# Moving second-stage transposes one piece ahead in an embedding-interaction kernel, with warm-up matmuls and a reordered one-hot

## The chip, the cores and the metric

One core of one Trainium2 chip runs the kernel. The metric is device time in microseconds of one execution; lower is better. Inputs lie in HBM before the clock starts, and the output (512 numbers) is written back to HBM.

## The reference

A batch of 512 samples has 128 dense features and 26 table indices each. Every index picks a row of 128 numbers out of its table, so a sample has 26 embedding vectors and, with the dense features, 27 vectors. All their pairwise dot products feed a small tower of three layers:

```python
e = stack([tbl_f[ids[:, f]] for f in range(26)], axis=1)      # 512 x 26 x 128
sd = einsum('bfd,bd->bf', e, dense)                            # 26 per sample
ss = einsum('bfd,bgd->bfg', e, e); pairs = ss[:, iu, ju]       # 325 per sample
h = concat([dense, sd, pairs, dense], axis=1)                  # 512 x 607
h = maximum(h @ W_top1 + b_top1, 0)                            # 607 -> 512
h = maximum(h @ W_top2 + b_top2, 0)                            # 512 -> 256
y = h @ W_top3                                                 # 256 -> 1
```

## The kernel before

The kernel writes each engine's instruction stream by hand and ties them with semaphores. It has two stages.

**Gathers.** Sixteen of the tables (MAIN) are read row by row with indirect DMAs issued by GpSimd (POOL), line 294. There are 64 of them, four for each of 16 blocks of 32 samples, called b0 to b15. They land in the ring `rows`, which holds three blocks; the gathers of block n+3 wait until the transposes of block n are done (`filled`, line 293). TensorE (PE) then transposes the four 128x128 pieces of a block against the identity `ident` into a PSUM bank `stage` (function `transposes`, line 325), and ScalarE (ACT) copies them into the big table of vectors `ET` (`empty_stage`, line 470). The two stage banks are used in turn.

**Look-ups, first stage.** The other ten tables (ONE, about 1000 rows each) are loaded whole by SyncE's queue (SP). ACT casts each table to an upper part (`upper_part`, lines 457 and 459), VectorE (DVE) makes the rest, the lower part (`lower_part`, "split", line 558), and one-hot matrices of the indices (`make_onehot`, line 552). PE multiplies them (`look_up`, line 342). The tables come in six groups, SIDE = [[0],[1,2],[3,4],[5,6],[7,8],[9]], and each group takes eight chunks k = 0..7; a chunk is two matmuls of 512 columns for each table of the group. The results go by turns to the banks `gram` and `hidden`, and ACT takes them out (`take_look_up`, lines 480, 482). The dictionary AMID (line 200) says after which chunk (group, k) PE places the transposes of the dense features and of b0 to b7. ACT's stream follows the same dictionary.

**Second stage.** The samples are cut into nine pieces p: seven of 64 samples, two of 32. `gram_piece` (line 371) multiplies each sample's 27 vectors by themselves, 32x27 results a sample; the trace shows two matmul records for each, so 128 a piece of 64. DVE and ACT move the result from PSUM to `Z` (lines 568 and 492), DVE folds it with a mask (579, 586), and `layers(p)` runs the part of layers 1 and 2 (lines 387, 398, 413, 415) whose inputs are ready: nothing for p = 0 and 1, two columns of layer 1 from p = 2 on, layer 2 one piece later. Layer 3 is line 599 on DVE. The order on PE in piece p is: gram_piece(p), the transposes in SOON[p], layers(p), the transposes in LATER[p] (lines 429 to 435). A gram piece waits until ACT has emptied the stage bank of its last block (line 353); its first one waits for the last look-up (line 355).

The two dictionaries of the second stage are:

```python
SOON = {1: ["b8"], 2: ["b9"], 3: ["b10"], 4: ["b11"], 5: ["b12"]}
LATER = {5: ["b13"], 6: ["b14"], 7: ["b15"]}
```

At the start ACT's queue issues three small DMAs, the last of them (line 505) the bias of layer 1, transposed on the way in elements of four bytes. DVE's order in a group g of two tables is: both splits, then the eight one-hots (lines 615 to 619).

Of the kernel before, what the change touches and what calls it, by code (L numbers as in the profile page):

```python
# [11 lines left out]
P = 128  # L12
# [7 lines left out]
HC = H1 // P  # L20
# [14 lines left out]
KR = 8  # L35
RAW = 3

SIDE = [[0], [1, 2], [3, 4], [5, 6], [7, 8], [9]]
RING = 8


BS = 32
# [32 lines left out]
def group_of(i):  # L75

    return next(g for g, side in enumerate(SIDE) if i in side)
# [29 lines left out]
def dlrm_tower(nc, x, out):  # L107
    ctx = ExitStack()
    with ctx:
        def sb(name, shape, dt=F32):  # L110
            return ctx.enter_context(nc.sbuf_tensor(name, shape, dt))

        def pb(name, shape):
            return ctx.enter_context(nc.psum_tensor(name, shape, F32))

        def sem(name):
            return ctx.enter_context(nc.semaphore(name))
# [10 lines left out]
        part = sb("part", [P, 4, 2, KR * D], FP32R)  # L128
        onehot = sb("onehot", [P, RING, 2 * B], FP32R)
        ident = sb("ident", [P, P])  # L130
# [5 lines left out]
        b1c = sb("b1c", [P, HC])  # L136
# [12 lines left out]
        second = [pb(f"second{i}", [P, 512]) for i in range(2)]  # L149
# [11 lines left out]
        w1d_in = sem("w1d_in")  # L161
# [7 lines left out]
        ident_ready = sem("ident_ready")  # L169
# [28 lines left out]


        AMID = {(0, 7): ["dense"], (1, 3): ["b0"], (2, 1): ["b1"], (2, 5): ["b2"], (3, 1): ["b3"],  # L200
                (3, 6): ["b4"], (4, 3): ["b5"], (4, 7): ["b6"], (5, 7): ["b7"]}

        SOON = {1: ["b8"], 2: ["b9"], 3: ["b10"], 4: ["b11"], 5: ["b12"]}
        LATER = {5: ["b13"], 6: ["b14"], 7: ["b15"]}
        STAGED = [s for g, k in sorted(AMID) for s in AMID[g, k]] + [s for n in range(NP) for s in SOON.get(n, []) + LATER.get(n, [])]

        def bank_of(name):

            return stage[STAGED.index(name) % 2]

        def filled(name):

            return staged, STAGED.index(name) + 1
# [5 lines left out]
        def look_banks(g):  # L219

            return [b[:, :] for b in (gram if g % 2 == 0 else hidden)]
# [87 lines left out]
        def _(pe):  # L309
# [18 lines left out]
            def look_up(g):  # L328
# [4 lines left out]
                for k in range(KR):  # L333
                    pe.wait_ge(onehot_ready, KR * g + k + 1)
                    for j, i in enumerate(SIDE[g]):
# [5 lines left out]
                        for n in range(2):  # L341
                            last = pe.matmul(look_banks(g)[j], part[:, i % 4, n, D * k:D * (k + 1)],  # L342
                                             onehot[:, (KR * g + k) % RING, B * j:B * (j + 1)],
                                             start=(k == 0 and n == 0), stop=(k == KR - 1 and n == 1))
# [74 lines left out]
            def layers(p):  # L419

                for t, c in layer2_of(p):
                    layer2(t, c)
                for t, c in layer1_of(p):
                    layer1_dense(t, c)
                    layer1(t, c)

            for g in range(len(SIDE)):
                look_up(g)
            for p in range(NP):
                gram_piece(p)  # L430
                for name in SOON.get(p, ()):
                    transposes(name)
                layers(p)
                for name in LATER.get(p, ()):
                    transposes(name)
# [12 lines left out]
        @block.scalar  # L448
        def _(act):
            def upper_part(i):  # L450

                act.wait_ge(table_in[i], 16)
                if i >= 4:

                    act.wait_ge(chunk_done, KR * (group_of(i - 4) + 1))
                if i == 0:
                    act.copy(part[:, 0, 0, 2 * D:], raw[:, 0, 2 * D:]).then_inc(hi_ready, 1)
                else:
                    act.copy(part[:, i % 4, 0, :], raw[:, i % RAW, :]).then_inc(hi_ready, 1)  # L459

            def empty_stage(name):

                act.wait_ge(*filled(name))
                bank = bank_of(name)
                if name == "dense":
                    act.copy(denseT[:, :], bank[:, :])
                    act.copy(ETv[:, :, DENSE], bank[:, :]).then_inc(stage_taken, 1)
                else:
                    n = int(name[1:])
                    act.copy(ETv[:, BS * n:BS * (n + 1), 0:NM],  # L470
                             bank[:, :].rearrange("d (b v) -> d b v", v=NM)).then_inc(stage_taken, 1)

            def take_look_up(g):

                act.wait_ge(chunk_done, KR * (g + 1))
                for j, i in enumerate(SIDE[g]):
                    if i == NO - 1:

                        for at in (slice(0, P), slice(P, B)):
                            act.copy(ETv[:, at, V_ONE[i]], look_banks(g)[j][:, at]).then_inc(look_taken, 1)  # L480
                    else:
                        act.copy(ETv[:, :, V_ONE[i]], look_banks(g)[j]).then_inc(look_taken, 1)  # L482

            def move_gram(p):
                act.wait_ge(gram_done, p + 1)
                t = PIECES[p][0] // P
                if t >= ZT:

                    act.wait_ge(h1_done, HC * (t - ZT + 1))
                for i in (2, 3):  # L490
                    for dst, src in z_moves(p, (i,)):
                        last = act.copy(dst, src)  # L492
                    if i == 2:
                        for name in SOON.get(p, ()):
                            empty_stage(name)
                last.then_inc(gram_act, 1)

            def take_odd(t, c):

                act.wait_ge(h1_done, HC * t + c + 1)  # L500
                act.activation(h1T[:, t % 2, c, :], layer1_bank(t, c), ACT.Relu, bias=b1c[:, c:c + 1]).then_inc(h1_odd, 1)  # L501

            act.dma_start(rowid[:, :], x["rowid"]).then_inc(rowid_in, 16)
            act.dma_start(b2s[:, :], x["b_top2"].rearrange("(o n) -> o n", o=1)).then_inc(b2_in, 16)
            act.dma_start(b1c[:, :], x["b_top1"].rearrange("(c p) -> p c", p=P), allow_slow_non_contiguous=True).then_inc(w1d_in, 16)
            act.wait_ge(dve_consts, 1)
            act.activation(warm[:, :], zero[:, :], ACT.Identity, bias=zero[:, :])
            act.wait_ge(b2_in, 16)
            act.copy(b2h[:, 0, :], b2s[:, :]).then_inc(b2_high, 1)
            act.wait_ge(head_in, 16)  # L510
            act.copy(part[:, 0, 0, 0:2 * D], raw[:, 0, 0:2 * D]).then_inc(hi_ready, 1)
            for i in range(4):
                upper_part(i)
            for g in range(len(SIDE)):
                for k in range(KR):
                    if k == KR - 1:
                        take_look_up(g)
                    for name in AMID.get((g, k), ()):
                        empty_stage(name)
                for i in range(4, NO):  # L520
                    if group_of(i - 4) == g:
                        upper_part(i)
                if 1 <= g <= T:

                    t = g - 1
                    if t == 0:
                        act.wait_ge(look_taken, 3)
                        act.wait_ge(*emptied("dense"))
                    of = ETv[:, P * t:P * (t + 1), :]
                    act.copy(of[:, :, NV:NV + 3], of[:, :, LATE:NV])  # L530
                    act.copy(of[:, :, NV + 3:VP], of[:, :, LATE:LATE + VP - NV - 3]).then_inc(et_again, 1)
            act.wait_ge(w1d_in, 32)
            for p in range(NP):
                move_gram(p)
                if layer1_of(p):
                    take_odd(*layer1_of(p)[1])
                for name in LATER.get(p, ()):
                    empty_stage(name)
            for c in (1, 3):
                take_odd(T - 1, c)  # L540

        @block.vector
        def _(dve):
            def make_onehot(g, k):
                m = KR * g + k
                if k == 0:
                    dve.wait_ge(ids_in[g], 16)
                if m >= RING:

                    dve.wait_ge(chunk_done, m - RING + 1)  # L550
                w = B * len(SIDE[g])
                dve.tensor_scalar(onehot[:, m % RING, 0:w], ids16[:, B * SIDE[g][0]:B * SIDE[g][0] + w],  # L552
                                  rowid[:, k:k + 1], None, ALU.is_equal).then_inc(onehot_ready, 1)
# [59 lines left out]
                make_onehot(0, k)  # L613

            for g in range(1, len(SIDE)):
                for i in SIDE[g]:
                    lower_part(i, slice(0, KR * D)).then_inc(lo_ready, 1)
                for k in range(KR):
                    make_onehot(g, k)
            dve.wait_ge(b2_high, 1)  # L620
            dve.tensor_tensor(b2h[:, 1, :], b2s[:, :], b2h[:, 0, :].bitcast(F32), ALU.subtract).then_inc(b2_low, 1)
# [69 lines left out]
```

## Time and profile before

| what | value |
| --- | --- |
| median of three runs | 132.18 us (131.85 to 134.35) |
| the profiled execution's own time | 132.72 us |
| its span, first to last instruction | 130.9 us |
| PE busy / DVE / ACT / POOL | 94.0 / 73.7 / 61.8 / 67.5 us |
| mean granted TensorE clock | 0.896 of full |

The span is what the trace shows; 1.8 us of the execution's own time lie around it. PE's busy time includes matmuls that overlap, so it isn't PE at its peak. "Issue" is time in which an engine waited for nothing that the profile shows.

### The profile page before, as it was taken

How to read it: one execution, taken by the hardware profiler on the slowest of the kernel's cores; microseconds unless marked ns; L12 is line 12 of the kernel's file. 1: busy time of each engine (PE TensorE's matmuls, PEld its weight loads, DVE VectorE, ACT ScalarE, POOL GpSimd, SP SyncE). 2: the span in 40 equal slices, each digit the busy share in tenths (PEclk: the TensorE clock that was granted, in tenths of full speed). 3: DMA queues.
4: the chain of work that ended last, by engine and by line, in shares of the span. 5: the costliest groups of instructions: out<-in, count | busy, mean ns of one | idle time of the engine just before them, and what ended most of it. 6: DMA issues, size and time to landing. Idle time of an engine off the chain costs nothing.

```text
span 130.9 us, 3331 instructions
## 1 busy us (share of the span) xinstructions
PE 94.0 (72%) x1420; PEld 78.2 (60%) x1420; DVE 73.7 (56%) x170; ACT 61.8 (47%) x131; POOL 67.5 (52%) x70
## 2 busy tenths in 40 slices
PE   0089899999969999000547459397784997897892
PEld 0157688888858887000436349286674796786780
DVE  1387999999997835000008927264370731974621
ACT  3435591966908506300308909164370904964410
POOL 2878888787888787770831725538172560000000
PEclk9999999999999999965557756999999559999999
DMA  2999965947996121220110110102011110000000
GB/s 53 242 379 367 272 242 185 267 115 179 381 372 207 44 60 40 63 59 21 44 41 8 45 40 25 49 16 60 25 38 43 25 40 25 0 5 0 8 0 1
DMA packets 6849, 13.37 MB, mean 102 GB/s; under 512 B 2353, under 2 KB 3506, under 8 KB 6834
## 3 DMA queue, kind: packets, MB, share of 16 engines
q1 hardware_dynamic: 4112, 8.95, 21.4%
q0 software_dynamic: 2048, 4.20, 11.2%
q8 instruction: 11, 0.18, 0.6%
q10 hardware_dynamic: 674, 0.01, 0.3%
q14 instruction: 4, 0.03, 0.1%
HBM read 13.15 MB, written 0.00 MB: 100 GB/s over the span
## 4 chain that ended last, share of the span: by engine, by line
PE 44%; POOL 17%; issue 15%; DMA 7%; another core or an unknown queue 6%; ACT 6%; DVE 2%; DVEq 0%; ACTq 0%
POOL rows L294 17%; PE gram L371 12%; PE hidden L398 8%; PE second L415 6%; PE gram L342 6%; DMA rows<-in_tables_gather,idx 5%; PE stage L325 5%; PE hidden L387 3%; PE hidden L342 2%; ACT Z L492 2%; ACT ET L470 2%; ACT ET L482 2%; PE second L413 2%; DVE Z L568 2%
## 5 line engine op out<-in xcount | busy, mean ns | idle before, releaser
L294 POOL DMA_INDIRECT rows<-in_tables_gather,idx x64 | 66.8, 1044 | 39.0 <-issue 17.4
L568 DVE COPY Z<-gram 32x112 f32<-32x112 f32 (+3 forms) x72 | 23.0, 320 | 35.5 <-PE gram L371 34.6
L371 PE MATMUL gram<-ET 128*32 128x27 f32 x1024 | 17.0, 207 | 25.8 <-issue 12.8
L492 ACT COPY Z<-gram 32x112 f32<-32x112 f32 (+1 forms) x72 | 23.2, 322 | 23.7 <-PE gram L371 22.9
L371 PEld LDWEIGHTS gram<-ET 128*32 128x32 f32 x1024 | 14.1, 123 | 29.4 <-issue 26.0
L552 DVE TENSOR_SCALAR onehot<-ids,rowid 128x1024 fp32r<-128x1024 int16 (+1 forms) x48 | 28.7, 659 | 5.1 <-DMA ids<-in_ids_one 2.1
L342 PE MATMUL gram<-onehot,part 128*128 128x512 f32 x80 | 22.5, 434 | 6.6 <-DVE part L558 6.2
L342 PEld LDWEIGHTS gram<-onehot,part 128*128 128x128 f32 x80 | 16.4, 211 | 10.7 <-DVE onehot L552 6.2
L342 PE MATMUL hidden<-onehot,part 128*128 128x512 f32 x80 | 19.7, 397 | 0.6 <-issue 0.6
L342 PEld LDWEIGHTS hidden<-onehot,part 128*128 128x128 f32 x80 | 14.6, 188 | 3.7 <-issue 0.8
L558 DVE TENSOR_TENSOR part<-raw,part 128x1024 fp32r<-128x1024 f32 (+2 forms) x11 | 12.1, 1123 | 3.1 <-issue 2.4
L398 PE MATMUL hidden<-Z,W1s 128*128 128x128 f32 x84 | 13.2, 301 | 0.6 <-DVE Z L579 0.6
L398 PEld LDWEIGHTS hidden<-Z,W1s 128*128 128x128 f32 x84 | 12.2, 219 | 0.8 <-DVE Z L579 0.8
L459 ACT CAST part<-raw 128x1024 fp32r<-128x1024 f32 x9 | 9.4, 1070 | 5.2 <-DMA raw<-in_tables_one 4.3
L470 ACT COPY ET<-stage 128x512 f32<-128x512 f32 x16 | 9.5, 592 | 4.8 <-issue 4.6
L325 PE MATMUL stage<-ident,rows 128*128 128x128 f32 x64 | 10.8, 295 | 1.0 <-DMA rows<-in_tables_gather,idx 1.0
L415 PE MATMUL second<-W2s,h1T 128*128 128x256 f32 x32 | 10.2, 436 | 0.0
L325 PEld LDWEIGHTS stage<-ident,rows 128*128 128x128 f32 x64 | 8.0, 150 | 2.5 <-issue 1.4
L482 ACT COPY ET<-gram 128x512 f32<-128x512 f32 x5 | 5.3, 1145 | 6.9 <-PE hidden L342 5.6
L415 PEld LDWEIGHTS second<-W2s,h1T 128*128 128x128 f32 x32 | 5.8, 206 | 1.6 <-ACT h1T L501 0.4
L501 ACT ACTIVATE h1T<-hidden,b1c 128x128 f32<-128x128 f32 x7 | 2.6, 367 | 7.3 <-PE hidden L398 7.2
L387 PE MATMUL hidden<-denseT,W1e 128*128 128x128 f32 x28 | 6.0, 306 | 0.0
(38 smaller groups left out, 42.2 us busy)
## 6 DMA issues: line engine op xcount, KB each, us to landing
raw<-in_tables_one SPq DMA_DIRECT2D x9, 512.0 KB
ids<-in_ids_one SPq DMA_DIRECT2D x4, 256.0 KB, 5.5
rows<-in_tables_gather,idx POOLq DMA_INDIRECT x64
W1s<-in_W_pairs SPq DMA_DIRECT2D x1, 768.0 KB
W1d<-in_W_dense SPq DMA_DIRECT2D x1, 512.0 KB
W2s<-in_W_top SPq DMA_DIRECT2D x1, 512.0 KB
raw<-in_tables_one SPq DMA_DIRECT2D x1, 384.0 KB
ids<-in_ids_one SPq DMA_DIRECT2D x2, 128.0 KB, 3.6
```

The source lines that it names most:

```text
L294: pool.indirect_dma_start(out=rows[:, m % ROWS_RING, :], out_offset=None, in_=x["tables_gather"], in_offset=bass.IndirectOffsetOnAxis(ap=i ...
L325: last = pe.transpose(bank[:, P * k:P * (k + 1)], rows[:, (GB * n + k) % ROWS_RING, :], ident[:, :])
L342: last = pe.matmul(look_banks(g)[j], part[:, i % 4, n, D * k:D * (k + 1)], onehot[:, (KR * g + k) % RING, B * j:B * (j + 1)], start=(k == ...
L371: last = pe.matmul(gram[p % 2][32 * i:32 * i + 32, NV * j:NV * (j + 1)], ET[:, VP * b:VP * (b + 1)], ETv[:, b, 0:NV], start=True, stop=True)
L387: pe.matmul(layer1_bank(t, c), W1e[:, P * c:P * (c + 1)], denseT[:, P * t:P * (t + 1)], start=True, stop=False)
L398: last = pe.matmul(layer1_bank(t, c), W1s[:, s, P * c:P * (c + 1)], Z[:, t % ZT, s, :], start=False, stop=(s == 0))
L415: last = pe.matmul(at, h1T[:, t % 2, c, :], W2s[:, c, :], start=False, stop=(c == HC - 1))
L470: act.copy(ETv[:, BS * n:BS * (n + 1), 0:NM], bank[:, :].rearrange("d (b v) -> d b v", v=NM)).then_inc(stage_taken, 1)
L492: last = act.copy(dst, src)
L552: dve.tensor_scalar(onehot[:, m % RING, 0:w], ids16[:, B * SIDE[g][0]:B * SIDE[g][0] + w], rowid[:, k:k + 1], None, ALU.is_equal).then_inc ...
L558: return dve.tensor_tensor(part[:, i % 4, 1, cols], raw[:, i % RAW, cols], part[:, i % 4, 0, cols].bitcast(F32), ALU.subtract)
L568: last = dve.tensor_copy(dst, src)
```

## The change

Five edits. (1) PE runs ten 128x128 matmuls of the identity with itself before the first look-up. (2) The bias of layer 1 is laid out by the host as it stands in SBUF, so its DMA is a plain one. (3) In a group of two tables DVE makes the one-hot of chunk 0 between the two splits. (4) The transposes of b4, b5 and b6 move to later chunks of the look-ups. (5) In the second stage the transposes of b8 to b13 stand behind the gram pieces 0 to 5, one piece earlier each; b13, which stood behind layers(5), now stands ahead of them. b14 and b15 stay.

```diff
+WARM = 10
         AMID = {(0, 7): ["dense"], (1, 3): ["b0"], (2, 1): ["b1"], (2, 5): ["b2"], (3, 1): ["b3"],
-                (3, 6): ["b4"], (4, 3): ["b5"], (4, 7): ["b6"], (5, 7): ["b7"]}
-
-        SOON = {1: ["b8"], 2: ["b9"], 3: ["b10"], 4: ["b11"], 5: ["b12"]}
-        LATER = {5: ["b13"], 6: ["b14"], 7: ["b15"]}
+                (4, 1): ["b4"], (4, 4): ["b5"], (5, 1): ["b6"], (5, 7): ["b7"]}
+
+        SOON = {p: [f"b{p + 8}"] for p in range(6)}
+        LATER = {6: ["b14"], 7: ["b15"]}
...
+            pe.wait_ge(ident_ready, 1)
+            for n in range(WARM):
+
+                pe.matmul(second[0][:, 0:P], ident[:, :], ident[:, :], start=True, stop=True)
             for g in range(len(SIDE)):
                 look_up(g)
...
-            act.dma_start(b1c[:, :], x["b_top1"].rearrange("(c p) -> p c", p=P), allow_slow_non_contiguous=True).then_inc(w1d_in, 16)
+            act.dma_start(b1c[:, :], x["b_top1"]).then_inc(w1d_in, 16)
...
             for g in range(1, len(SIDE)):
-                for i in SIDE[g]:
+                for n, i in enumerate(SIDE[g]):
                     lower_part(i, slice(0, KR * D)).then_inc(lo_ready, 1)
-                for k in range(KR):
+                    if n == 0:
+
+                        make_onehot(g, 0)
+                for k in range(1, KR):
                     make_onehot(g, k)
...
-        "b_top1": np.ascontiguousarray(inputs["b_top1"]), "W_top2": np.ascontiguousarray(inputs["W_top2"]),
+        "b_top1": np.ascontiguousarray(np.asarray(inputs["b_top1"]).reshape(HC, P).T), "W_top2": np.ascontiguousarray(inputs["W_top2"]),
```

## Rows read from the trace of the kernel before

**Rows 1.** The page, busy tenths in 40 slices of 3.27 us, and TensorE's granted clock.
```profile
PE   0089899999969999000547459397784997897892
POOL 2878888787888787770831725538172560000000
PEclk9999999999999999965557756999999559999999
```

**Rows 2.** The waits: engine, line, waited for; us in total, times, longest.
```profile
PE gram L371 <- issue: 12.8, 20, 1.2
...
POOL rows L294 <- PE stage L325: 17.0, 5, 4.6
...
POOL rows L294 <- remote: 3.0, 1, 3.0
```

**Rows 3.** POOL's timeline, first gather of a block: start, us, what, idle before.
```profile
71.41 0.94 POOL L294 DMA_INDIRECT rows<-in_tables_gather,idx  x1 [4.56 <-PE stage L325]
...
79.62 0.94 POOL L294 DMA_INDIRECT rows<-in_tables_gather,idx  x1 [3.52 <-PE stage L325]
...
87.06 0.94 POOL L294 DMA_INDIRECT rows<-in_tables_gather,idx  x1 [2.75 <-PE stage L325]
...
102.62 0.94 POOL L294 DMA_INDIRECT rows<-in_tables_gather,idx  x1 [3.36 <-PE stage L325]
```

**Rows 4.** Windows, line 371 alone: span, PE and PEld busy (records), clock, DMA, GB/s.
```profile
62.17:66.85 4.68, 2.36 (x67) 1.61 (x67) 0.50 0.18 46
66.85:71.41 4.56, 2.72 (x189) 2.73 (x189) 0.62 0.07 20
...
79.62:84.31 4.69, 1.23 (x46) 0.76 (x46) 0.90 0.17 45
...
99.25:102.62 3.37, 1.01 (x87) 0.98 (x87) 0.77 0.10 24
102.62:107.31 4.69, 0.00 (x0) 0.00 (x0) 0.50 0.17 42
```

**Rows 5.** PE's timeline in the second stage.
```profile
62.35 0.85 PE L371 MATMUL gram<-ET 128*32 128x27 f32 x46 [10.01 <-ACT ET L480]
...
67.84 2.72 PE L371 MATMUL gram<-ET 128*32 128x27 f32 x189 [1.12 <-issue]
...
86.72 0.50 PE L413 MATMUL second<-b2h,ones 1*128 1x256 f32 x2
...
89.99 0.50 PE L371 MATMUL gram<-ET 128*32 128x27 f32 x34
...
100.29 1.01 PE L371 MATMUL gram<-ET 128*32 128x27 f32 x87 [1.20 <-issue]
...
102.28 0.79 PE L413 MATMUL second<-b2h,ones 1*128 1x256 f32 x2
...
108.09 0.60 PE L325 MATMUL stage<-ident,rows 128*128 128x128 f32 x4
109.36 1.29 PE L371 MATMUL gram<-ET 128*32 128x27 f32 x128 [0.68 <-ACT ET L470]
```

**Rows 6.** PE's timeline in the look-ups.
```profile
6.23 2.05 PE L342 MATMUL gram<-onehot,part 128*128 128x512 f32 x4 [6.23 <-DVE part L558]
...
38.49 0.63 PE L325 MATMUL stage<-ident,rows 128*128 128x128 f32 x4 [1.03 <-DMA rows<-in_tables_gather,idx]
...
51.74 0.60 PE L325 MATMUL stage<-ident,rows 128*128 128x128 f32 x4
```

**Rows 7.** ACT's timeline at the end of the look-ups.
```profile
50.38 2.05 ACT L482 COPY ET<-gram 128x512 f32<-128x512 f32 x2 [5.63 <-PE hidden L342]
...
61.87 1.08 ACT L480 COPY ET<-hidden 128x128 f32<-128x128 f32 x2 [8.22 <-remote]
```

**Rows 8.** DVE's timeline, second split of group 1.
```profile
12.44 1.22 DVE L558 TENSOR_TENSOR part<-raw,part 128x1024 fp32r<-128x1024 f32 x1 [0.73 <-issue]
```

**Rows 9.** The chain in order of time: start, us, what.
```profile
105.08 0.43 PE hidden L387 x2
```

## The prediction

> **What bounds the kernel now.** I read the busy tenths first, then the waits, then PE's and POOL's timelines side by side. The tenths [rows 1] show three parts: look-ups with a dense PE to about 52 us, an empty PE for three slices, and a second stage from 62 us in which PE is half busy and POOL works in bursts. The granted clock falls to half twice, around 57 to 80 us and at 101 to 108 us, each time after PE had been thin or idle.
>
> In the second stage two waits are large and belong together [rows 2]. POOL waits 17.0 us in all, five times, for PE's transposes: a block of gathers may start only when the block three before it is transposed. And PE's gram matmuls have 12.8 us of idle "issue", in 20 gaps, for which no semaphore is to blame. Laid on top of each other, the timelines say what the gaps are. The windows in [rows 4] have POOL's bursts as their boundaries. A burst is four gathers and takes 4.68 us. While one runs, a gram piece gets through its first 34 to 47 records at a free pace and then nearly stops (46 in all in 79.62:84.31, 67 in the first burst); with POOL idle 189 pass in 2.72 us. Behind the first burst, which ends at 66.85, the gram runs free again at 67.84; behind the fifth, which ends at 99.25, at 100.29 [rows 4, 5]. The three between are the same: 0.97 to 1.04 us behind the burst's end, five times out of five. The wide matmuls of the layers don't stop so: in 102.62:107.31 POOL gathers, PE has no gram, and the layers run through.
>
> So the second stage is one loop over two engines. Transposes of a block release a burst (4.68), the gram piece that falls beside it is held to burst end + 1.0, its rest takes about 1, its transposes and the wake-up of POOL 0.85 (full clock) or 1.32 (half). The loop's period is what [rows 3] show: 8.21, 7.44, then 7.51, then 8.05 us (102.62 - 87.06 = 15.56 for the last two). Two things escape the loop now. Piece 1 follows piece 0 in the same free run of 189 records, beside no burst. And the last burst (b15's gathers, from 102.62) lies beside layers(5).
>
> In front of it, PE's last look-up record and b7's transposes end at 52.34 [rows 6], but ACT takes the last table only at 61.87 [rows 7], and POOL, which needs b7's transposes, is held 3.0 us until 62.17 [rows 2]. Group 4's result too is taken late, at 50.38 after 5.63 us of waiting [rows 7], though the records have group 5's matmuls running from 48 us on. PE's completions reach the others late here, and they all come through once POOL has gone quiet at 62.17 - 3.0 = 59.17. The records don't say why. I take it for the same coupling of PE to the gathers as in the gram.
>
> **The change part by part.** The sum is made against the span of the profiled execution, 130.9 us, whose own time is 132.72; that is 0.54 above the median of 132.18, so a difference is added to the median.
>
> *Second-stage transposes one piece ahead.* Call X the start of the first burst of this stage (now 62.17). Piece 0 is unchanged: it ends at X + 6.77 (68.94 now: 4.68 + 0.99 + 61 records in 1.10). Today piece 1 follows at once. After the change b8's transposes do, and POOL's next burst starts at X + 6.77 + 1.32 = X + 8.09, instead of X + 9.24. That is 1.15 us earlier, and it is the gain. The price is that piece 1 now runs beside this burst. It has at most 0.3 us before POOL wakes, some 20 records, and then the usual 46; it needs 128, so it is held. Then each piece has a burst:
> - to b8's burst: 8.09
> - piece 1, no layers beside it, as piece 2 today: 8.21
> - piece 2, no layers between it and its burst, the same: 8.21
> - piece 3: 7.44; piece 4: 7.51
> - piece 5 to its end: 8.05 - 1.32 = 6.73
> Together X + 46.2 for the end of piece 5, which today is at 101.30 = X + 39.1. From there to piece 6, today takes 8.06 (101.30 to 109.36): b12's transposes, layers(5) 102.28 to 108.09, b13's transposes and 0.68 of waiting for ACT to copy them [rows 5]. Afterwards b13's are the only ones and ACT's copy lies beside layers(5): transposes 0.6 (full) to 1.05 (half) and layers 3.3 (as 86.72 to 89.99, full clock) to 5.8 (half, as now). I take the middle, 5.4, because today's half clock there comes after a thin piece 5 and the new piece 5 is as thin, but starts from another moment. So piece 6 starts at X + 51.6, against X + 47.2 now: +4.4, with ends +2.9 and +5.9. A few tenths come back because piece 1 starts with some records done: -0.2. From piece 6 on nothing is changed; b14 and b15 stay where they were.
>
> *Look-ups.* b4's transposes wait 1.03 us for their gathers [rows 6]; three chunks later they don't: -1.03 on PE, or nothing if the engine behind it is late. The one-hot between the splits fills DVE's idle 0.73 before the second split [rows 8], one one-hot being 0.66: PE can begin group 1 with the first table, and DVE, which is busy without a gap from there to 42 us, is 0.66 earlier throughout. The ten identity matmuls: the nearest row has two records (one such matmul) in 0.43 us at half clock [rows 9], so 4.3 us from about 1.5, done at 5.8, and PE has nothing to do until 6.23 anyway [rows 6]. Ends: +0.5 if they run over, and at best they let group 0 run at full clock (its first four took 2.05 us, half a microsecond each, where a pair of records is half as long at full clock); but group 1 can't be complete before its second split, 12.44 + 1.22 = 13.66 [rows 8], so that up to 2 us gained in group 0 become 0.7 at most behind it. The bias DMA falls from elements of 4 bytes; bounds 0 to -0.3 on the first table's arrival. Together PE's look-ups end 1.3 to 3 us earlier.
>
> What of it arrives? X doesn't hang on PE's records but on when the completions come through, and they do when POOL goes quiet. POOL is busy without a gap from 3 to 59 us at its own pace and isn't sped up by any edit. Two ways: completions come through as now, a little sooner because fewer are left: X -0.3 to -1. Or b6, now two chunks later, is still outstanding when POOL wants it, one burst and a start ahead of 59.17, at 54.48. Then POOL goes quiet there for 1 to 2 us, everything comes through, and b7 never holds it: its two bursts follow each other and X falls at 60.5 to 61.5. No lateness at all would give 59.47, the lowest X can be: -2.7. I take -1.2; the range is 0 to -2.7.
>
> Sum: +4.4 - 0.2 - 1.2 = +3.0 us. Span 133.9, own time 135.7, against the median 135.2. A measurement of this kernel can tell about 2%, 2.6 us, from no change.
>
> The Trainium skill (SBUF — State Buffer, section "SBUF: two separate sides") says that DMA ports and engine ports are disjoint, that a DMA can't be slowed by a compute operation nor the other way round, and that PE never waits on anyone. By that rule the gaps of rows 4 would have another cause and piece 1 would stay as cheap as it is. The trace speaks against it with five coincidences of 1.0 us, so the sum doesn't use it; it is the second rival's ground.
>
> **The rivals.**
> *A. Piece 1 slips through.* If the hold needs more of POOL's burst than I think (in piece 0 the free pace ends at 63.20, 1.03 us behind the burst's start) and piece 1's 128 records, 1.84 us at the free pace, are nearly out by then, b9's transposes follow at once and two bursts run back to back beside piece 2. Piece 2 then ends at X + 8.09 + 9.7 + 2.0 = X + 19.8 instead of X + 23.2. That is -3.4, so -0.4 in all: 131.8. For it: piece 1 starts ahead of the burst. Against: pieces 0 and 2 to 5 stop after 34 to 47 records wherever they start in the burst, so it is a count and not a time.
> *B. The gaps aren't tied to the gathers (the faster side).* Then the transposes ahead cost nothing, POOL's 17.0 us of waiting shrink, b13's 0.68 us of waiting for ACT goes, and the look-ups' 1.3 to 3 us reach X. Gain 2.9 to 4.6: about 128.5. If the late completions vanish too, up to 8 us more. It decides if the windows with gathers show piece 1 complete. Against it stand rows 4.
> *C. Nothing arrives from the look-ups and layers(5) run at half clock:* +5.9 - 0.2 = +5.7, 137.9; the forecast's upper end.
>
> **How the numbers follow.** Forecast with its clock variants 0.55 (its own range 133.5 to 137.9), A and mixtures near no change 0.25, B 0.2. Slower by over 2% is over 134.8: 0.43, from most of the forecast. Faster by over 2%: 0.19, B. Within: 0.38. The range goes from 129.5, which leaves out the better half of B, to 138.0.
>
> **What would show it.** Right: piece 1 stops after 46 to 80 records and runs free 1.0 us behind the end of b11's gathers; six bursts of which five gate a gram piece behind piece 0; POOL's last burst starts near 100, and PE's piece 6 behind 111; POOL's waiting for transposes falls while gram's "issue" grows by about 4 us. The first burst of the stage starts near 61. PE's first table starts at 6.2 still, group 1 before 14.38, no wait of b4's transposes. Wrong: piece 1's records within 2.5 us of each other beside gathers, or X below 59.4, or completions of the look-ups that come in time.

## The result, and the profile after

The changed kernel has a median of 137.55 us (135.84 to 139.52, four runs) beside 132.3 us for the kernel before. The ratio is 1.033, with a 95% interval of 1.020 to 1.045: slower, by over 2%. Two of the four runs, the profiled one among them (138.0 us), lie over 1.5% above the fastest and aren't in the ratio; the granted clock of all four is the same to 0.003. The forecast was 135.2 us and slower. By the ratio the forecast's own baseline of 132.18 becomes 136.5, which is 1.3 us above the forecast; the median is 2.35 above it. Both are inside the range.

The page: busy tenths of PE and POOL in 40 slices (now 3.41 us each) and the granted clock, to lay beside [rows 1].

```profile
PE   5966999999999964221194755949787799988893
...
POOL 2887877887878878777227073553727000000000
PEclk9999999999999998555555555699999856999999
```

PE's empty stretch of three slices has become a thin one of five (the digits 4 2 2 1 1), and the clock is at half for 34 us in a row (nine slices and parts of the two around them), where it had two shorter spells of 13.6 and 6.8 us; then once more, as before, beside layers(5). The waits, to lay beside [rows 2]:

```profile
PE gram L372 <- issue: 23.2, 35, 1.9
...
POOL rows L295 <- PE stage L326: 16.8, 5, 4.8
```

The gram's idle "issue" went from 12.8 to 23.2 us, while POOL's waiting for transposes stayed where it was (17.0 to 16.8), though the edit meant to release POOL earlier. PE's timeline shows both halves of the story.

```profile
1.52 4.45 PE L431 MATMUL second<-ident 128*128 128x128 f32 x20 [1.52 <-POOL ident L302]
5.92 1.16 PE L343 MATMUL gram<-onehot,part 128*128 128x512 f32 x4
...
52.36 0.63 PE L326 MATMUL stage<-ident,rows 128*128 128x128 f32 x4 [2.48 <-DMA rows<-in_tables_gather,idx]
52.92 0.57 PE L372 MATMUL gram<-ET 128*32 128x27 f32 x41
...
68.12 1.01 PE L372 MATMUL gram<-ET 128*32 128x27 f32 x58 [1.20 <-issue]
...
70.11 1.24 PE L372 MATMUL gram<-ET 128*32 128x27 f32 x51
...
76.08 1.01 PE L372 MATMUL gram<-ET 128*32 128x27 f32 x57 [0.51 <-issue]
...
108.36 0.79 PE L414 MATMUL second<-b2h,ones 1*128 1x256 f32 x2
...
114.50 1.42 PE L372 MATMUL gram<-ET 128*32 128x27 f32 x128
```

The look-ups did become faster. The ten identity matmuls end as the first table is ready, the first four look-up matmuls take 1.16 us in place of 2.05 (the granted clock reads 1.00 there in both traces, so that this is the clock is my reading and not in the rows), and b7's transposes have to wait 2.48 us for their gathers. Piece 0 starts at 52.92, 9.4 us earlier than in the trace of before [rows 5]. And it ends at 69.14, where before it ended at 68.94: 41 records at once, then a trickle for 14 us, then the rest. What was new behind it is piece 1: 51 records from 70.11, a halt, the last 57 from 76.08. Before, it had gone through in a single free run with the end of piece 0 [rows 5, the 189 records]. More than half of the growth of the gram's "issue" time isn't the change's: the kernel before, traced again as e5, has 19.1 us of it.

POOL's timeline gives the new loop, to lay beside [rows 3], and the windows of line 372 (the gram) with a burst and without one, to lay beside [rows 4]:

```profile
70.46 0.94 POOL L295 DMA_INDIRECT rows<-in_tables_gather,idx  x1 [4.80 <-PE stage L326]
...
78.42 0.94 POOL L295 DMA_INDIRECT rows<-in_tables_gather,idx  x1 [3.25 <-PE stage L326]
...
101.17 0.94 POOL L295 DMA_INDIRECT rows<-in_tables_gather,idx  x1 [2.72 <-PE stage L326]
```

```profile
60.97:65.66 4.69, 0.77 (x7) 0.59 (x7) 0.50 0.22 56
65.66:70.46 4.80, 1.56 (x84) 1.48 (x87) 0.50 0.08 19
70.46:75.16 4.70, 2.38 (x62) 1.58 (x54) 0.50 0.17 42
75.16:78.42 3.26, 1.56 (x83) 1.24 (x85) 0.50 0.11 25
```

In the burst from 60.97 the gram gets seven records done, in the next quiet 84, then 62, then 83. The bursts start 7.96, 7.99, 7.36 and 7.40 us apart, and now the last of the five, at 101.17, also has a gram piece beside it.

### The profile page after: what moved, and what is told of

It is laid out like the page before. It is cut to its first block, busy times and chain, and to the rows that moved or that the text cites. A ratio compares the mean times of both kernels' runs of the same rounds, so it can differ in the third digit from the quotient of the medians.

```text
span 136.2 us, 3371 instructions
## 1 busy us (share of the span) xinstructions
PE 101.9 (75%) x1440; PEld 83.2 (61%) x1440; DVE 73.7 (54%) x170; ACT 61.8 (45%) x131; POOL 68.9 (51%) x70
## 4 chain that ended last, share of the span: by engine, by line
PE 40%; POOL 27%; issue 25%; DMA 3%; DVE 2%; ACT 1%; DVEq 0%
POOL rows L295 27%; PE gram L372 16%; PE hidden L399 8%; PE second L416 6%; PE stage L326 5%; PE hidden L388 2%; DMA rows<-in_tables_gather,idx 2%; PE second L414 1%; DVE Z L573 1%; DMA idg<-in_ids_gather 1%; PE stage L399 1%; ACT ET L475 1%; DVE h2w L604 0%; DVE Z L584 0%; DVE idx L611 0%
## 5 line engine op out<-in xcount | busy, mean ns | idle before, releaser
L295 POOL DMA_INDIRECT rows<-in_tables_gather,idx x64 | 68.2, 1066 | 36.2 <-issue 17.7
L497 ACT COPY Z<-gram 32x112 f32<-32x112 f32 (+1 forms) x72 | 23.2, 322 | 38.8 <-PE gram L372 38.0
L372 PE MATMUL gram<-ET 128*32 128x27 f32 x1024 | 21.9, 209 | 24.7 <-issue 23.2
L372 PEld LDWEIGHTS gram<-ET 128*32 128x32 f32 x1024 | 16.4, 124 | 31.1 <-issue 28.6
L343 PE MATMUL gram<-onehot,part 128*128 128x512 f32 x80 | 20.2, 398 | 1.1 <-DVE onehot L557 1.1
L343 PEld LDWEIGHTS gram<-onehot,part 128*128 128x128 f32 x80 | 14.6, 188 | 4.5 <-DVE onehot L557 1.6
L326 PE MATMUL stage<-ident,rows 128*128 128x128 f32 x64 | 11.5, 308 | 2.5 <-DMA rows<-in_tables_gather,idx 2.5
L487 ACT COPY ET<-hidden 128x512 f32<-128x512 f32 x4 | 4.2, 1170 | 4.9 <-PE hidden L343 4.9
```

The costliest lines, as they stand in the source:

```text
L295: pool.indirect_dma_start(out=rows[:, m % ROWS_RING, :], out_offset=None, in_=x["tables_gather"], in_offset=bass.IndirectOffsetOnAxis(ap=i ...
L326: last = pe.transpose(bank[:, P * k:P * (k + 1)], rows[:, (GB * n + k) % ROWS_RING, :], ident[:, :])
L372: last = pe.matmul(gram[p % 2][32 * i:32 * i + 32, NV * j:NV * (j + 1)], ET[:, VP * b:VP * (b + 1)], ETv[:, b, 0:NV], start=True, stop=True)
```

## The experiments

All kernels are changed from the one before or the one after as said. Chips differ, so each ratio is to the kernel before on the same chip; its medians were 132.3 (the result), 132.17 and 132.94 (one chip, runs e1 to e8), 133.79 (e9 to e11), and 108.31 (e12), of which more below.

**e1, the second-stage edit alone; e2, the four others alone.** Each is one half of the diff: e1 has SOON and LATER of after in the kernel before, e2 has SOON and LATER of before in the kernel after.

```diff
-        SOON = {1: ["b8"], 2: ["b9"], 3: ["b10"], 4: ["b11"], 5: ["b12"]}
-        LATER = {5: ["b13"], 6: ["b14"], 7: ["b15"]}
+        SOON = {p: [f"b{p + 8}"] for p in range(6)}
+        LATER = {6: ["b14"], 7: ["b15"]}
```

Expected of e1:

> The kernel before with the second-stage edit alone (b8 to b13 one piece earlier). Theory (a gram piece beside a burst of gathers is held until the burst is over, and now piece 1 has a burst too): look-ups and the first burst as before, X near 62; the five bursts behind it start 7.4 to 8.2 us apart, piece 5 ends near X + 45.5, piece 6 starts near 114, span about 136, time 136 to 138, ratio 1.03 to 1.045. Rival (the loss comes from the look-up edits, the second stage is neutral or a gain): 130 to 132.5.

Expected of e2:

> The kernel after with the second-stage order of before, so the four other edits alone. Theory: the look-ups end near 50 and the first burst starts near 61 as in the kernel after, piece 0 is held until POOL is quiet and ends near 69, piece 1 runs through beside no burst in 1.8 us, b8's transposes release POOL near 72, as before the change; time 131.5 to 133.5, no change within 1%. Rival (the look-up edits carry the loss): 135 to 138. Rival (the 9 us that the look-ups gain arrive): under 128.

Measured: e1 136.55 us, ratio 1.039 (1.023 to 1.055). e2 134.24 us, ratio 1.026 (1.014 to 1.037). The second-stage edit alone makes a loss as large as the whole one. The two halves together, 3.9 and 2.6%, are more than the whole, 3.3%; the kernel after wasn't run on their chip, so how they add isn't known. PE's timeline of e1:

```profile
52.87 0.56 PE L371 MATMUL gram<-ET 128*32 128x27 f32 x41
...
67.84 0.89 PE L371 MATMUL gram<-ET 128*32 128x27 f32 x47 [0.50 <-issue]
...
69.71 1.24 PE L371 MATMUL gram<-ET 128*32 128x27 f32 x51
...
75.69 1.05 PE L371 MATMUL gram<-ET 128*32 128x27 f32 x58 [1.09 <-issue]
```

Piece 1 is held as in the kernel after, and this with look-ups that nobody touched. Yet here too piece 0 starts at 52.87. So the late completions that I read out of the trace of before aren't a property of its look-ups. For e2 none of the three guesses came true: it is neither within 1%, nor over 135 us, nor a gain, but 2.6% slower (between 1.4 and 3.7%). Where that may come from is looked at below (e8 to e10).

**e5, the kernel before once more**, to settle that.

> The kernel before, once more, for its trace. Theory: the late completions at the end of the look-ups (ACT's last take at 61.87) are a matter of the single execution, since the second-stage edit alone, with the same look-ups, showed none (last take at 52.5): here too the first piece starts near 52.9, the first burst near 61, piece 0 ends near 69 and piece 1 near 72; time 131 to 134. Rival (they belong to this kernel): last take near 62 again.

Measured 131.91 us, span 130.1. ACT takes the last table in time, and the first burst starts at 60.45:

```profile
51.85 1.06 ACT L480 COPY ET<-hidden 128x128 f32<-128x128 f32 x2 [0.75 <-PE hidden L342]
```

```profile
52.37 0.56 PE L371 MATMUL gram<-ET 128*32 128x27 f32 x41
...
67.44 2.58 PE L371 MATMUL gram<-ET 128*32 128x27 f32 x174 [0.50 <-issue]
69.95 0.66 PE L325 MATMUL stage<-ident,rows 128*128 128x128 f32 x4
```

The ten lost microseconds in front of the gram [rows 7] belonged to that one execution, and they cost next to nothing: the two traces of one kernel differ by 10 us in the start of piece 0 and by 0.6 us in its end. The trace of before also keeps each update of the semaphore that ACT waits for. The last PE look-up record ends at 51.9, but the updates stand at 53.24, 55.35, 57.47, 59.62, 61.06, 61.77, 61.81 and 61.85: about 2.1 us apart beside the gathers, and the last four within 0.8 us behind them. In e5 the last one is at 51.83. So in that execution it was the completions of the wide look-up matmuls that trickled, as the small ones of the gram do in the others.

**e3, no gathers for b11 to b15.** The transposes of these blocks read what lies in the ring; 20 of 64 gathers are left out, and PE's waits for them.

```diff
-            for n in range(NB):
+            for n in range(11):
...
-                    pe.wait_ge(gathered[n], 16 * GB)
+                    if n < 11:
+                        pe.wait_ge(gathered[n], 16 * GB)
```

> The kernel after without the gathers of b11 to b15 (their transposes read what lies in the ring). Theory: once the burst of b10 is over, no gram piece is held; pieces 1 to 5 take 1.8 us each beside about 0.6 of transposes and 2.4 to 3.3 of layers, piece 6 starts near 94 instead of 114.5, span about 116. Rival (the gaps in the gram belong to PE itself, its instruction supply or its clock): gaps of 0.7 us stay in every piece and the span stays above 130.

Measured 120.42 us, span 118.2, piece 6 at 95.8. PE's timeline:

```profile
68.63 1.19 PE L373 MATMUL gram<-ET 128*32 128x27 f32 x70 [0.50 <-issue]
...
70.80 1.91 PE L373 MATMUL gram<-ET 128*32 128x27 f32 x123
...
73.78 1.19 PE L373 MATMUL gram<-ET 128*32 128x27 f32 x117
77.55 0.31 PE L373 MATMUL gram<-ET 128*32 128x27 f32 x11 [2.58 <-issue]
```

No trickle anywhere behind piece 0; piece 1 takes 2.4 us instead of 7.0. Between the two spans, 136.2 and 118.2, lie 18 us that hang on five bursts, the half clock beside them included (mean granted clock 0.850 and 0.926; one run each). The rival is right in one detail: a gap of 2.58 us in piece 2 and one of 0.84 in piece 3 are left without a gather in sight.

**e4, a ring of six blocks.** If POOL's 17 us of waiting were the cost, this would be the cure.

```diff
-ROWS_RING = 3 * GB
+ROWS_RING = 6 * GB
```

> The kernel after with a ring of six blocks of rows in place of three, so POOL needn't wait for transposes until b14. Theory: POOL gathers without a gap until b13 (about 80 us), piece 0 is held all that time and ends near 82; then two held pieces, then free ones; piece 6 near 115 to 118, time 137 to 141, no gain although POOL's 17 us of waiting are mostly gone. Rival (POOL's waiting for transposes is what costs): piece 0 done by 70 and the time under 130.

Measured 145.04 us, ratio 1.102 (1.093 to 1.111). POOL's waits for transposes fell to 10.6 us, and the kernel became 10% slower, more than the theory had. Windows of the gram, and PE's timeline:

```profile
53.10:80.90 27.80, 3.85 (x62) 2.71 (x63) 0.54 0.20 53
80.90:86.90 6.00, 2.00 (x66) 1.39 (x66) 0.50 0.04 11
```

```profile
85.73 1.08 PE L372 MATMUL gram<-ET 128*32 128x27 f32 x62 [0.45 <-issue]
```

In 27.8 us beside uninterrupted gathers PE did 62 records. This isn't PE short of instructions: the DMA queues of the same 27.8 us show one 16 KB packet of the instruction queue, from 53.7 to 55.0, and none in the 6 us behind, in which 66 more records pass.

```profile
q8 instruction: 1, 0.02, 0.3%
```

And PE ran free again only 4.84 us behind the last gather, at 80.89. That gap is no constant 1.0 us as I had it, it grows with the time that the piece stood beside gathers:

| kernel | piece 0 beside gathers, us | free again behind the last, us |
| --- | --- | --- |
| before, first trace (62.35 to 66.86) | 4.5 | 1.0 |
| e6 (53.26 to 61.01) | 7.8 | 1.9 |
| e5, before again (52.37 to 65.16) | 12.8 | 2.3 |
| after (52.92 to 65.65) | 12.7 | 2.5 |
| e4 (53.16 to 80.89) | 27.7 | 4.8 |

The other traces with 12.7 us beside gathers scatter from 2.2 (e1, e8) to 3.2 us (e10), so the length isn't all; still none of them is near 1.0 or 4.8. This is how a backlog behaves that is worked off once the gathers stop. What it is a backlog of, the traces don't say.

**e6 and e7, is it the bytes, POOL, or the indirect gather?** In both the gathers of b10 to b15 become plain DMAs of as many other rows, the same bytes: in e6 on SyncE's queue, in e7 still on POOL's.

```diff
+                if n >= 10:
+                    pool.dma_start(rows[:, m % ROWS_RING, :], x["tables_gather"][P * m:P * (m + 1), :]).then_inc(gathered[n], 16)
+                    return
                 pool.indirect_dma_start(
```

Expected of e6:

> The kernel after with the gathers of b10 to b15 replaced by plain DMAs of as many rows on SyncE's queue (other rows of the tables, same bytes), POOL idle from then on. Theory (what holds the gram is POOL at work on gathers): piece 0 runs free about 1 to 4 us after POOL's last burst, near 60 to 64, no later piece is held, span about 110 to 116. Rival (the transfers themselves hold the gram): pieces 1 to 5 are held as long as their four transfers last, 2 to 5 us each, span over 122.

Expected of e7:

> The kernel after with the gathers of b10 to b15 replaced by plain DMAs of as many rows, still on POOL's queue. Theory (POOL's making of each transfer holds the gram, whatever its kind): pieces 0 to 5 are held as in the kernel after, for as long as POOL's bursts last. Rival (only indirect gathers do it): no piece held behind b9's burst, span as with SyncE's queue.

Measured: e6 112.51 us, e7 114.53 us. Here my theory fell in its wording: not POOL at work, only POOL at work on indirect gathers. POOL's timeline of e7, and PE's windows of the gram for piece 1, beside such transfers, and for piece 3, beside none:

```profile
66.34 2.13 POOL L296 DMA_DIRECT2D rows<-in_tables_gather  x4 [2.42 <-PE stage L329]
```

```profile
65.97:68.29 2.32, 1.84 (x128) 1.63 (x128) 0.79 0.18 49
...
76.21:77.85 1.64, 1.64 (x128) 1.54 (x128) 0.71 0.15 40
```

Four plain transfers from POOL take 2.1 us, and piece 1 does its 128 records beside them in 2.3. The same bytes by another kind of DMA don't hold the gram. Nor is it the queue or its packets: e7's transfers from 66.34 are 96 packets of 0.20 MB on queue q0, and the gathers of the kernel before in 62.17 to 66.85 are 95 of 0.20 MB on the same queue. What differs is POOL's own time on them, 2.1 us for four in place of 4.7; which part of an indirect gather holds PE wasn't taken further apart.

**e8, e9, e10: what the front edits cost.** e8 is the kernel before with the ten identity matmuls; e9 is e2 with eight of them; e10 is e2 with none.

```diff
-WARM = 10
+WARM = 8
```

Expected of e8:

> The kernel before with the ten identity matmuls alone. Theory (the start is hidden, group 0 is faster but group 1 waits for the second split): PE ends its look-ups 0 to 0.7 us earlier, POOL's own pace sets the first burst, no change: 131 to 133. Rival (it is the warm-up that makes the four front edits 2.6% slower, by what it leaves behind on PE): 133.5 to 135.5.

Expected of e9:

> The four front edits with the order of the second stage of before, and eight identity matmuls in place of ten: PE's stream is four weight loads and four matmul records shorter ahead of piece 1. With ten, the last record of piece 1 came 1.2 us behind the rest, while a 16 KB packet of the instruction queue was on its way (started at 69.97, piece 1's free run ended at 71.15). Theory (PE had run out of instructions one record ahead of the piece's end): the boundary moves behind piece 1, the gap at its end is gone, b8's transposes end near 71.9 in place of 73.14; time 0.5 to 1.5 us under that of the four front edits, 133 to 133.8. Rival (the gap has to do with the hold by the gathers and comes back whatever the count): piece 1's last record again over 1 us late, time 134.2 or more.

Expected of e10:

> The front edits without the identity matmuls, the order of the second stage of before. Theory (the instruction boundaries lie as in the kernel before, and what the look-ups gain is swallowed by the hold of piece 0): no gap at the end of piece 1, PE's look-ups end near 51, the first burst near 60.7, time within 0.7% of before, 132 to 133.2. Rival (moving b4 to b6 or the one-hot costs POOL time, since its gathers of b6 and b7 took 5.8 us a burst in the front-edit kernel and 4.9 before): first burst 0.7 us or more later than before's 60.45, time 133.5 or more.

Measured: e8 133.31 us, ratio 1.011 (0.998 to 1.024), unclear. e9 135.35 us, 1.014 (1.008 to 1.020), by the time the rival. e10 134.52 us, 1.006 (1.002 to 1.011); its first burst starts at 61.05, 0.6 us later than in e5, between the theory and the rival, and its time is the rival's. The end of piece 1 and b8's transposes in e2, then in e9:

```profile
68.38 2.77 PE L372 MATMUL gram<-ET 128*32 128x27 f32 x188 [1.20 <-issue]
72.37 0.18 PE L372 MATMUL gram<-ET 128*32 128x27 f32 x1 [1.22 <-issue]
72.50 0.65 PE L326 MATMUL stage<-ident,rows 128*128 128x128 f32 x4
```

```profile
69.39 2.87 PE L372 MATMUL gram<-ET 128*32 128x27 f32 x194 [0.50 <-issue]
72.19 0.90 PE L326 MATMUL stage<-ident,rows 128*128 128x128 f32 x3
73.51 0.48 PE L326 MATMUL stage<-ident,rows 128*128 128x128 f32 x1 [0.42 <-issue]
```

In e2 the very last record of piece 1 comes 1.22 us behind the others. A look at the DMA queues in 69.9 to 71.2 us of e2 shows one 16 KB packet of the instruction queue under way:

```profile
q8 instruction: 1, 0.02, 4.3%
```

With eight instructions less ahead of it (four weight loads and four matmul records), as expected, the gap leaves piece 1. But it doesn't go: it comes exactly four records later, inside b8's transposes, whose four records take 1.8 us in place of 0.6. e8, with as many instructions on PE as e2, has it where e2 has it: 1.40 us ahead of the last record of piece 1.

The gaps of e3, e6 and e7 are of the same kind. All three stand at the same record, with 11 left in piece 2, and e3's and e6's next one comes 126 records later (33 left in piece 3), which is 252 weight loads and matmuls, about one 16 KB packet. Each has a 16 KB packet of the instruction queue within 1 us of PE's stop, and PE goes on 1.3 to 1.5 us after its end:

| kernel | packet of the instruction queue | PE goes on at |
| --- | --- | --- |
| e2 | 69.97 to 70.86 | 72.37 |
| e9 | 70.94 to 72.13 | 73.51 |
| e8 | 69.41 to 70.58 | 72.11 |
| e3 | 75.18 to 76.11 | 77.55 |
| e6 | 68.90 to 70.24 | 71.53 |
| e7 | 69.83 to 71.13 | 72.46 |

So it reads as an instruction stream run dry by a gram piece that goes through too fast; where PE is slower, such packets pass without a gap (69.49 to 70.49 in the trace of after).

What the gap costs is another matter. From the first burst to the end of b8's transposes it is 11.97 us in e2, 12.16 in e9 and 10.16 in e5, which looks like the gap's price. But e10, which has no gap there, takes 11.82: its gram runs free 3.2 us behind the burst in place of e5's 2.3, and b8's transposes take 1.12 us in place of 0.66. So the gap isn't shown to be what makes the front edits slower. e2's profiled execution has a span of only 1.0 us over e5's, so its trace can account for a third of the 2.6% at most, and the cause of e2's loss stays open. The order of the ratios, 1.026, 1.014 and 1.006 for ten, eight and none, fits a price for the warm-up, but it mixes two chips.

**e11, the kernel after without the warm-up.**

> The kernel after without the identity matmuls. Theory (the second-stage edit carries the loss of 3 to 4%, the warm-up at most 1%): 135.5 to 137, ratio to before 1.025 to 1.04, pieces 1 and 2 held as in the kernel after. Rival (the warm-up carries half of the loss): 134 or less.

Measured 140.05 us, ratio 1.052 (1.046 to 1.058). Both were wrong in the time; pieces 1 and 2 were held as said. In the whole change the warm-up seems not to cost but to give: without it the loss is 5.2%, with it 3.3%, but on another chip. The bursts of e11 are as far apart as in the kernel after (8.10, 8.12, 7.45 and 7.53 us for 7.96, 7.99, 7.36 and 7.40); what is longer is layers(3), 94.70 to 99.63, partly at half clock (4.9 us for 3.3). I have no run of both on one chip, so how much of the 1.9% is the warm-up stays open.

**e12, the other way round.** If bursts hold the gram and not the layers, transposes later than before should gain a little. Those of b8, b9 and b10 move one piece later; b11 and b12 stay, and b13 goes ahead of layers(5), as in the change.

```diff
-        SOON = {1: ["b8"], 2: ["b9"], 3: ["b10"], 4: ["b11"], 5: ["b12"]}
-        LATER = {5: ["b13"], 6: ["b14"], 7: ["b15"]}
+        SOON = {2: ["b8"], 3: ["b9"], 4: ["b10", "b11"], 5: ["b12", "b13"]}
+        LATER = {6: ["b14"], 7: ["b15"]}
```

> The kernel before with the second-stage transposes moved the other way: b8 behind piece 2, b9 behind 3, b10 and b11 behind 4, b12 and b13 behind 5. Theory (a burst holds the gram piece beside it and not the layers): pieces 1 and 2 run free behind piece 0, piece 2 done near 73; pieces 3 and 4 are held once each, piece 5 by two bursts in a row (9.7 us and then 1.5 to 2 more); from X to piece 6 about 46 to 47.5 us against 48.1 in the trace of before taken again; time 0.5 to 1.5% under before. Rival (POOL's order matters only by how early the gathers are done): 5 us later throughout, ratio 1.03 or more.

Measured 113.0 us, ratio 1.045 (1.039 to 1.052). The ratio isn't the news: on this chip the kernel before takes 108.31 us (eleven runs, 107.4 to 109.83), 24 us less than on the others. The windows have the bursts of b8 to b13 as their boundaries; the gram alone:

```profile
51.77:56.46 4.69, 2.11 (x147) 1.73 (x148) 1.00 0.22 59
56.76:61.61 4.85, 2.72 (x223) 2.33 (x224) 1.00 0.23 59
61.91:66.60 4.69, 0.84 (x90) 0.73 (x85) 0.66 0.23 59
66.91:71.60 4.69, 0.72 (x32) 0.42 (x22) 1.00 0.22 59
71.90:76.60 4.70, 1.70 (x128) 1.38 (x128) 1.00 0.23 59
76.90:81.59 4.69, 1.87 (x128) 1.51 (x128) 1.00 0.24 59
```

Whole pieces of 128 records go through beside gathers of the same kind, bytes and pace: on this chip there is no hold. (Its gaps, up to 57.07, 60.57 and 68.33, all end 1.5 us behind a 16 KB packet of the instruction queue.) So on this chip e12 couldn't test its theory. The trace shows a plainer reason for its loss; the kernel before has no trace on this chip to lay beside it. PE is through piece 5 before POOL has the rows:

```profile
79.75 0.66 PE L325 MATMUL stage<-ident,rows 128*128 128x128 f32 x4
83.30 1.09 PE L325 MATMUL stage<-ident,rows 128*128 128x128 f32 x4 [2.89 <-DMA rows<-in_tables_gather,idx]
84.32 0.79 PE L413 MATMUL second<-b2h,ones 1*128 1x256 f32 x2
...
89.77 1.82 PE L371 MATMUL gram<-ET 128*32 128x27 f32 x128
```

b13's transposes, set ahead of layers(5), wait 2.89 us for their gathers, the layers stand behind them, and the clock falls to half for most of them: 5.45 us in place of the 3.3 that such layers take at full clock. The two make 5.0 us, and the loss is 4.7. POOL never waits here for PE (its waits are 63 pauses of 0.3 us), so up to there it is POOL's pace that bounds the second stage.

## Why the prediction was right

**The forecast mechanism held.** Piece 1 was held beside b11's gathers after 51 records; b14's and b15's bursts, too, stood beside gram pieces; e1 shows the loss with this edit alone and e3 shows that it hangs on the gathers. POOL's waiting didn't fall as "What would show it" had it: 16.8 for 17.0 us, or for the 17.4 of e5. What an earlier release saved was waited for again, since one more of the pieces that POOL waits for was now held. The gram's "issue" did grow by about the 4 us forecast if it is laid beside e5, 19.1 to 23.2 us; the 12.8 of [rows 2] came from the execution whose piece 0 started late.

**The terms of the sum**, from the trace of after, which has a span of 136.2 us against the forecast's 133.9:
- X: forecast -1.2, measured 60.97 - 62.17 = -1.2. The size is right by luck. I expected a gain from the look-ups, and there was none: beside e5, the same kernel without the accident, X is 0.5 us later (60.97 for 60.45). What is gone is the lateness of completions, 3.0 us of POOL's waiting that belonged to one execution, but POOL's bursts for b6 and b7 took 5.83 and 5.63 us, where the trace of before had 4.91 and 5.13, so X didn't come down to 59.47.
- Piece 0: forecast X + 6.77, measured X + 8.17. This is the term that was mis-sized, +1.4. I took "burst end + 1.0" as a constant; it is longer where the piece has stood beside gathers for longer, here 2.5 us.
- The loop's five periods to the end of piece 5 without the first: 38.1 forecast, 107.72 - 70.46 = 37.3 measured, -0.8.
- Piece 5 to piece 6: forecast 5.4 as a middle, measured 6.8, +1.4. layers(5) ran at half clock, as at the forecast's upper end.
- The 0.2 for piece 1's early start and the tail behind piece 6 come to +0.3 together.
The differences sum to +2.3, the 136.2 - 133.9 of the spans.

**The look-up edits** did what was said on PE (2.0 us earlier at 49.88, forecast 1.3 to 3) and arrived nowhere, for the reason given: POOL sets X. What I hadn't thought of is that 40 more instructions on PE move the places at which its instruction supply runs out. By e2, on its chip, the front edits cost 2.6% where I had them gain; no run shows what of them does.

**The rivals.** A, piece 1 slipping through, fell on the count of 51, which is what had spoken against it. C gave the clock of layers(5) right, and C's other half, that nothing arrives from the look-ups, is what e5 says. The gain of 2.9 to 4.6 us that B was given can't be added up from its terms: 0.68 and 1.3 to 3 make 2.0 to 3.7. B was told as the rule of the Trainium skill (SBUF — State Buffer, "SBUF: two separate sides"), that a DMA doesn't slow a compute engine. On three groups of runs the rows contradict what it would make of the gram; on e12's chip they agree with it, with 128 records in a burst. The page speaks of SBUF's ports, and no run shows that the hold is there. So B is wrong for the kernel as it was measured, and right for a chip that this study met once. I can't say what the change does there. Two things point different ways: the hold that made its price is absent, and b13 ahead of layers(5), which the change has too, cost 5 us in e12.

## What to carry to other kernels

Lay the busy bursts of one engine over the unexplained "issue" gaps of another before calling a wait the cost: here 17 us of POOL waiting looked like the thing to shorten, and both kernels that set out to shorten it (ring of six, transposes ahead) got slower, since what POOL did in its bursts stopped the engine that it waited for. Price an earlier release by what it then runs beside, not by the wait it ends. And take the kernel before to a second chip and a second trace before building on a large gap, or on a gain that rests on it: one 10 us gap was an accident of one execution, and 24 us of this kernel belong to some chips and not to another.

## What the runs showed of the hardware that I had not expected

- Indirect gathers from POOL (4.7 us for four) nearly stop a stream of small matmuls, 62 records in 27.8 us, on two chips and in the result's own runs; plain DMAs of the same bytes don't, from POOL (2.1 us for four) or from SyncE. The layers' wide matmuls weren't stopped (PE was busy for 4.69 of 4.69 us beside the last burst of before), but in one execution the completions of the last wide look-up matmuls trickled 2.1 us apart.
- The recovery takes longer the longer it lasted: 1.0 us after 4.5 us, 2.2 to 3.2 after 12.7, 4.8 after 27.7.
- One chip of those used doesn't show it at all; the same kernel takes 108.3 us there and 132 to 134 on the others. Every run lists its span and its clock, so every execution was being recorded; whether the hold exists in one that isn't recorded wasn't tried, and neither was the change on that chip.
- A gram piece at its free pace of 10 to 14 ns a record outruns PE's instruction supply: gaps of 0.4 to 2.6 us, 126 records apart, that end 1.3 to 1.5 us behind the packet of the instruction queue and move by four records when eight instructions are taken out ahead of them.
- Semaphore updates of PE can come up to 10 us late (the last at 61.85, with the last look-up record ending at 51.9) in one execution of a kernel and not in the next.
